# The experts' low-rank tile in four matmuls of 128 stationary columns, made one expert ahead

## What is computed

```python
xt = einsum('bct,bcd->bdt', x, cond_w[itok])               # 1024 tokens x 256
probs = softmax(xt @ gate_w); top_p, top_i = top_k(probs, 2)
for each of the two choices, each of 8 experts with at most 160 tokens per choice:
    h = gelu(buf @ w1[e] + b1[e])                          # 256 -> 1024
    y = h @ w2[e] + b2[e]                                  # 1024 -> 256
    y = y + gelu(buf @ wd[e]) @ wu[e]                      # the low-rank path, 256 -> 32 -> 256
    out[token] += y * weight
shared = gelu(xt @ sw1 + sb1) @ sw2 + sb2 + gelu(xt @ swd) @ swu
return x + out + 0.2 * shared
```

## Time and profile before

| what | us |
|---|---|
| median of the timed runs (3) | 177.4 |
| lowest and highest of them | 177.09 and 178.9 |
| the profiled execution, its own time | 177.45 |
| its span from the first to the last instruction | 175.6 |
| PE busy in the span | 169.9 |
| ACT busy | 140.5 |
| DVE busy | 144.1 |
| POOL busy | 96.8 |

### The profile page before, as it was taken

How to read it: one execution, slowest core, us unless ns; L and a number is a source line. 1 busy time by engine, 2 the same in 40 slices (tenths; PEclk the granted TensorE clock), 3 DMA queues, 4 the chain that set the end, 5 groups by cost and what they waited for, 6 DMA issues and landing times.

```text
span 175.6 us, 4118 instructions
## 1 busy us (share of the span) xinstructions
PE 169.9 (97%) x1442; PEld 164.3 (94%) x1442; DVE 144.1 (82%) x330; ACT 140.5 (80%) x315; POOL 96.8 (55%) x112
## 2 busy tenths in 40 slices
PE   5799999999999999999999999999999999999994
PEld 5666879999999999999999999999999999999993
DVE  3478999998695889989889699798988989889722
ACT  3277789407888998997899799999899999897920
POOL 5835348511547572097678858868837555074700
PEclk9999999999999999999999999999999999999999
DMA  4599100069929484595987768769778598776242
GB/s 127 163 350 349 41 2 4 7 175 299 362 56 318 103 304 111 194 252 79 307 252 117 275 193 157 213 197 234 194 255 185 144 312 164 247 247 78 30 90 67
DMA packets 25981, 31.84 MB, mean 181 GB/s; under 512 B 4668, under 2 KB 22488, under 8 KB 25960
## 3 DMA queue, kind: packets, MB, share of 16 engines
q1 hardware_dynamic: 21816, 26.22, 46.7%
q0 software_dynamic: 3904, 5.25, 17.0%
q10 hardware_dynamic: 240, 0.10, 0.2%
HBM read 26.31 MB, written 5.24 MB: 180 GB/s over the span
## 4 chain that ended last, share of the span: by engine, by line
PE 93%; DMA 5%; SPq 0%; DVE 0%; issue 0%; DVEq 0%
PE y_ps L1056 14%; PE y_ps L1057 14%; PE y_ps L1058 14%; PE hid_ps L1056 10%; PE hid_ps L1057 10%; PE hid_ps L1058 10%; DMA x_in<-in_x 5%; PE turn_ps L1056 4%; PE turn_ps L1058 4%; PE turn_ps L1057 4%; PE turn_ps L1235 3%; PE row_ps L1251 1%; PE hid_ps L1095 1%; PE y_ps L1195 1%; PE y_ps L1215 1%; PE y_ps L1251 0%
## 5 line engine op out<-in xcount | busy, mean ns | idle before, releaser
L495 POOL DMA_INDIRECT out_rows<-y_row,slot_tok x23 | 38.5, 1675 | 26.8 <-DVE y_row L946 11.6
L481 POOL DMA_INDIRECT slot_in<-slot_rows,slot_src x23 | 29.5, 1281 | 17.0 <-issue 6.1
L1056 PE MATMUL y_ps<-w_h,hid_h 128*128 128x256 f32 (+2 forms) x128 | 36.4, 285 | 0.0
L1057 PE MATMUL y_ps<-w_l,hid_h 128*128 128x256 f32 (+2 forms) x128 | 36.1, 282 | 0.0
L1058 PE MATMUL y_ps<-w_h,hid_l 128*128 128x256 f32 (+2 forms) x128 | 36.1, 282 | 0.0
L741 DVE TENSOR_TENSOR hid_l<-gelu_f,hid_h 128x320 fp32r<-128x320 f32 (+3 forms) x54 | 26.5, 500 | 8.0 <-ACT hid_h L643 7.5
L1056 PE MATMUL hid_ps<-xs_h,w_h 128*128 128x248 f32 (+6 forms) x96 | 27.6, 288 | 0.0
L1058 PE MATMUL hid_ps<-xs_h,w_l 128*128 128x248 f32 (+6 forms) x96 | 27.2, 284 | 0.0
L1057 PE MATMUL hid_ps<-xs_l,w_h 128*128 128x248 f32 (+6 forms) x96 | 27.2, 284 | 0.0
L718 DVE TENSOR_TENSOR w_l<-w_raw,w_h 128x512 fp32r<-128x512 f32 x40 | 26.7, 703 | 0.0
L643 ACT ACTIVATE hid_h<-hid_ps,bias_s 128x320 fp32r<-128x320 f32 (+2 forms) x48 | 26.4, 549 | 0.0
(11 more groups left out here) (260 smaller groups left out, 465.9 us busy)
## 6 DMA issues: line engine op xcount, KB each, us to landing
w_raw<-in_L_ffn_w SPq DMA_DIRECT2D x16, 1024.0 KB
w_raw<-in_L_ffn_sw SPq DMA_DIRECT2D x3, 1024.0 KB
x_in<-in_x SPq DMA_DIRECT2D x2, 512.0 KB, 4.1
w_raw<-in_L_ffn_sw SPq DMA_DIRECT2D x2, 512.0 KB, 6.5
slot_rows<-token_row SPq DMA_DIRECT2D x8, 128.0 KB, 5.1
wu_raw<-in_L_ffn_wu SPq DMA_DIRECT2D x24, 32.0 KB
out_rows<-base SPq DMA_DIRECT2D x1, 512.0 KB
slot_in<-slot_rows,slot_src POOLq DMA_INDIRECT x23
```

What stands on the lines that cost most here:

```text
L481: pool.indirect_dma_start(out=slot_in[par][0:n, s, :], out_offset=None, in_=x_rows, in_offset=bass.IndirectOffsetOnAxis(ap=slot_src[0:n, e ...
L495: pool.indirect_dma_start(out=out, out_offset=bass.IndirectOffsetOnAxis(ap=slot_tok[0:n, e, s:s + 1].bitcast(U32), axis=0), in_=y_row[0:n, ...
L1056: pe.matmul(out_ap, l_h, r_h, start=start, stop=False)
L1057: pe.matmul(out_ap, l_h, r_l, start=False, stop=False)
```

## The change

The low-rank tile leaves the hidden tiles of the experts (those of the shared expert stay as they were). `low_tile(e)` makes it in four matmuls: the stationary operand is 128 columns wide, two copies of the high part of `wd` and two of its low part, and both parts of the slots are streamed past it. Its 128 output rows hold the high products (rows 0 to 63) and the low products (64 to 127), which are still to be added. ACT copies the lower half to SBUF (`low_copy`), DVE adds the two (`low_sum`), ACT takes two gelus of the sum (`low_gelu_part`), DVE subtracts (`low_lo`).

The tile of expert e + 1 is made in period e, in PE's second pass of the second layer, ahead of feature tile 3 (`LOW_MADE_AT`); that of expert 0 at the start of period 0. ACT has the copy ahead of w2 chunk 2 (`LOW_COPY_AT`) and the gelus ahead of w2 chunk 3; DVE has the sum between w2 chunks 0 and 1 and the last subtraction after w2 chunk 2. The wait for `slots_lo` of the next expert moves from the head of the next period to `low_tile`. The two copies of `slots_hi_part` become one over both banks, as do the two subtractions of `slots_lo_part`. POOL makes the high part of `wd` ahead of the gather instead of after it, and waits for `low_made` there.

```diff
+LOW_COPY_AT = 2
+LOW_MADE_AT = 3
...
-        wd_h = [sb(f"wd_h{i}", [P, KD, 3, RANK], F32R) for i in range(2)]
-        wd_l = [sb(f"wd_l{i}", [P, KD, 3, RANK], F32R) for i in range(2)]
+        wd_s = [sb(f"wd_s{i}", [P, KD, 4, RANK], F32R) for i in range(2)]
...
+        low_sums = gelu_f[0:2 * RANK, 0:2, SLOTS:SLOTS + SLOTS // 2]
+        low_g = cond_g[0:RANK, :].rearrange("p (i n) -> p i n", i=2)[:, :, SLOTS:SLOTS + SLOTS // 2]
...
             def wd_hi_part(v, par):
-                if v >= 2:
-                    pool.wait_ge(hid_made, hid_before(v))
+                if v >= 3:
+                    pool.wait_ge(low_made, v - 2)
...
             def period(e, par):                                  # POOL
+                if e + 2 <= E:
+                    wd_hi_part(e + 2, par)
                 if e + 2 < E:
                     gather(e + 2, par)
-                if e + 2 <= E:
-                    wd_hi_part(e + 2, par)
...
+            def low_copy(e):
+                act.wait_ge(low_made, e + 1)
+                act.activation(low_sums, halves(turn_ps[0][2 * RANK:4 * RANK, 0:SLOTS]), ACT.Copy).then_inc(low_copied, 1)
+            def low_gelu_part(e):
+                act.wait_ge(low_summed, e + 1)
+                if e > 0:
+                    act.wait_ge(low_used, e)
+                    act.wait_ge(low_split, e)
+                act.activation(low_g, low_sums[0:RANK, :, :], ACT.Gelu)
+                act.activation(halves(low_s[0:2 * RANK, 0:SLOTS]), low_sums, ACT.Gelu).then_inc(low_gelu, 1)
...
             def slots_hi_part(n):
-                for k in range(KD):
-                    act.activation(xs_h[:, k, 0:n], turn_ps[k][:, 0:n], ACT.Copy).then_inc(slots_hi, 1)
+                act.activation(xs_h[:, :, 0:n], turn_both[:, :, 0:n], ACT.Copy).then_inc(slots_hi, 1)
...
             def period(e, par):                                  # ACT
-                for j in range(HT):
+                if e == 0:
+                    low_copy(0)
+                for j in range(1, HT):
                     gelu_tile(e + 2, j, MOST[e], lambda f: bias_s[:, e, f:f + 1])
+                    if e == 0 and j == 1:
+                        low_gelu_part(0)
...
                 for c in range(CHUNKS):
+                    if c == LOW_COPY_AT and e < E - 1:
+                        low_copy(e + 1)
+                    if c == CHUNKS - 1 and e < E - 1:
+                        low_gelu_part(e + 1)
                     w2_chunk(e + 2, par, c)
...
+            def low_sum(e):
+                dve.wait_ge(low_copied, e + 1)
+                dve.tensor_tensor(low_sums, halves(turn_ps[0][0:2 * RANK, 0:SLOTS]), low_sums, ALU.add).then_inc(low_summed, 1)
+            def low_lo(e):
+                dve.wait_ge(low_gelu, e + 1)
+                dve.tensor_tensor(halves(low_s[2 * RANK:LOW, 0:SLOTS]), low_g, halves(low_s[0:RANK, 0:SLOTS].bitcast(F32)),
+                                  ALU.subtract).then_inc(low_split, 1)
...
                 for c in range(CHUNKS - LATE_LO):                # DVE
+                    if c == LOW_COPY_AT - 1 and e < E - 1:
+                        low_sum(e + 1)
                     w2_chunk(c, par, e + 2)
+                if e < E - 1:
+                    low_lo(e + 1)
...
+            def low_tile(e, par, size):
+                pe.wait_ge(slots_lo, e + 1)
+                pe.wait_ge(wd_lo, e + 2)
+                for k in range(KD):
+                    both = wd_s[par][:, k, :, :].rearrange("p g r -> p (g r)")
+                    pe.matmul(turn_ps[0][:, 0:size], both, xs_h[:, k, 0:size], start=(k == 0), stop=False)
+                    ins = pe.matmul(turn_ps[0][:, 0:size], both, xs_l[:, k, 0:size], start=False, stop=(k == KD - 1))
+                ins.then_inc(low_made, 1)
...
                 for f in range(NF):                              # expert_out, and rows_out likewise
+                    if m == KD - 1 and f == LOW_MADE_AT:
+                        midway()
...
                 for e, size in enumerate(sizes):                 # experts
-                    pe.wait_ge(slots_lo, (e + 1) * KD)
-                    for j in range(HT):
+                    if e == 0:
+                        low_tile(0, other, size)
+                    for j in range(1, HT):
                         hidden(e + 2, j, other, e + 1, xs_h, xs_l, slice(0, size), size)
```

More of the change, by code:

```diff
@@ L84, in build @@
         y_ps = [bank(f"y_ps{i}") for i in range(2)]
-        turn_ps = [bank(f"turn_ps{i}") for i in range(2)]
+        turn_both = ctx.enter_context(nc.psum_tensor("turn_both", [P, KD, 512], F32))
+        turn_ps = [turn_both[:, k, :] for k in range(KD)]
         row_ps = bank("row_ps")
@@ L249, in build @@
         wu_lo = sem("wu_lo")
+        low_made = sem("low_made")
+        low_copied = sem("low_copied")
+        low_summed = sem("low_summed")
+        low_gelu = sem("low_gelu")
+        low_split = sem("low_split")
+        low_used = sem("low_used")
         hid_made = sem("hid_made")
@@ L334, in held_by @@
         def held_by(u, j):
-            tiles = [i for i in range(1 if u == LAST else 0, j) if hid_banks(u)[i] is hid_banks(u)[j]]
+            tiles = [i for i in range(0 if u < 2 else 1, j) if hid_banks(u)[i] is hid_banks(u)[j]]
             return tiles[-1] if tiles else None
@@ L921, in slots_lo_part @@
                 n = MOST[e]
[L922 to L925, removed]
+                dve.wait_ge(slots_hi, e + 1)
+                dve.tensor_tensor(xs_l[:, :, 0:n], turn_both[:, :, 0:n], xs_h[:, :, 0:n].bitcast(F32),
+                                  ALU.subtract).then_inc(slots_lo, 1)
             def weigh_rows(e, par):
@@ L1193, in expert_out @@
                 cols = slice(m * P, (m + 1) * P)
-                pe.wait_ge(hid_split, hid_count(e + 2, 0))
-                pe.matmul(dst, wu_s[par][:, cols], low_s[:, 0:size], start=True, stop=False)
+                pe.wait_ge(low_split, e + 1)
+                ins = pe.matmul(dst, wu_s[par][:, cols], low_s[:, 0:size], start=True, stop=False)
+                if m == KD - 1:
+                    ins.then_inc(low_used, 1)
                 for f in range(NF):
+                    if m == KD - 1 and f == LOW_MADE_AT:
+                        midway()
                     if m == 0:
@@ L1201, in expert_out, with rows_out @@
                 ins.then_inc(y_made, 1)
-            def rows_out(e, par, size):
+            def rows_out(e, par, size, midway):
                 v = e + 1
@@ L1214, in rows_out @@
                     cols = slice(s * P, s * P + n)
-                    pe.matmul(dst, low_s[:, cols], wu_s[par][:, :], start=True, stop=False)
+                    ins = pe.matmul(dst, low_s[:, cols], wu_s[par][:, :], start=True, stop=False)
+                    if s == tiles[-1]:
+                        ins.then_inc(low_used, 1)
                     for f in range(NF):
+                        if s == tiles[-1] and f == LOW_MADE_AT:
+                            midway()
                         if s == tiles[0]:
```

41 lines of the change are left out of this document (23 added, 18 removed).

## The result

The changed kernel takes 182.97 us in the median of four runs (182.04 to 185.47), the kernel before, beside it, 177.45: a ratio of 1.028 (1.018 to 1.037). It is slower, as forecast, and 182.0 was the forecast. One of the four runs, 185.47, is a slow one, and the ratio leaves it out. The profiled execution took 182.25 us with a span of 180.3, for 175.6 before: 4.7 us more.

The account below looks back on a forecast made before the run. PE was taken as the bound, busy 169.9 of 175.6 us, but the round through ACT and DVE would outlast its period. Waits of 6.46 less 1.92 for fewer matmuls add 4.54 to 177.45: 182.0 us, range 178.4 to 184.2.

Parts of the forecast that it names:

- waits forecast: PE's waits per period, for the next slots at `low_tile` and for ACT's copies at the transposes; sum 6.46 us.
- 1.92: PE's gain in us: six matmuls become four for eight experts, 16 fewer at 0.12 us each.
- The signs: PE idle before transposes (1.9 us in period 1, 0.2 after) and `low_tile` (0.4 to 1.1); ACT idle before new gelus.
- The wide operand: `low_tile`'s four matmuls with 128 stationary columns instead of 96 should cost the same 0.12 us each.
- The round of 3.52 us: From slots ready through DVE's sum, ACT's gelus and w2 chunk 3 to next gelu 1: 3.52 us; least trusted step.
- Period 0: `sort_biases` delays DVE's sum; PE waits 0.41 us for slots ready at 66.0, then 1.85 for results in period 1.
- Period 7: The last period loses six matmuls and is 0.72 us shorter, with no wait forecast.
- One copy for two saves nothing: Merged copy in `slots_hi_part`: no fixed part saved on ACT, 1.0 ns a column either way.
- POOL's `wd` first costs nothing: POOL making `wd` ahead of the gather is free: its slots are wanted only in period 2, past 85 us.
- A: Rival: PE is the bound and every wait stays covered, so faster, 175.5 us; chance 0.10.
- B: Rival: ACT never gets late, only 3.0 us of waits for the slots remain, 178.5 us; chance 0.10.
- C: Rival: period 1's 1.85 us of idle PE lets the granted clock fall, 185.6 us; chance 0.06.

Follow-up runs that it names:

- e10: e6 with the transposes of the results one hidden tile later (behind tile 3 instead of 2): 177.63 us, 0.996 of the kernel before.
- e1: Changed kernel with DVE's low-rank sum right behind w1 chunk 3, ahead of `sort_biases` and w2 chunk 0: 180.36 us, 1.0095 of the kernel before.
- 2: Changed kernel with the next slots ahead of w1 on ACT and DVE: 182.41 us, 1.020 of the kernel before.
- e9: Changed kernel with the transposes of the results behind hidden tile 3 instead of 2: 182.34 us, 1.028 of the kernel before.
- e6: e3 with DVE's low part of `wd` also ahead of the slots: 178.37 us, 0.994 of the kernel before.
- e7: e6 with POOL's gather ahead of `wd`'s high part again: 178.42 us, 0.995 of the kernel before.
- e3: Changed kernel with both the sum ahead of the w2 chunks and the slots ahead of w1: 179.33 us, 1.001 of the kernel before.
- e5: Changed kernel with `sort_biases` behind DVE's w2 chunks of period 0: 181.47 us, 1.017 of the kernel before.
- e12: e10 with hidden-tile gelus and subtractions only on the columns the matmuls use: 177.18 us, 0.990 of the kernel before.
- e4: Control: the kernel before the change with the slots ahead of w1: 178.03 us, 0.998 of the kernel before.
- e8: e7 with six matmuls instead of four for each low-rank tile: 177.73 us, 0.997 of the kernel before.

## Why the prediction was right

**The size.** 182.0 forecast for 182.25 of the profiled execution. By periods, each as the change of its length with the matmuls it lost or gained taken out (0.24; +0.24 in period 0), from the stretches shown and the earlier trace rows:

| period | waits forecast | measured |
|---|---|---|
| 0 | 0.41 | 0.04 |
| 1 | 2.45 | 2.36 |
| 2 | 0.22 | 0.04 |
| 3 | 0.74 | 0.73 |
| 4 | 0.95 | 0.91 |
| 5 | 1.09 | 1.16 |
| 6 | 0.60 | 0.74 |
| 7 | 0 | 0.53 |
| sum | 6.46 | 6.51 |

6.51 - 1.92 = 4.59, against the stretch's 4.58. That the totals agree within 0.05 is partly luck: periods 0 to 2 were forecast 0.64 us too long, and period 7 got 0.53 that was not forecast.

**The signs.** ACT's idle time before its new gelus was 2.04 us in period 0 and 0.42 to 0.47 after. PE's at `low_tile` was 0.30 to 0.64 us in five periods (forecast 0.4 to 1.1 in six). At the transposes PE waited in period 1 alone to speak of; in periods 3 and 4 they started 0.13 and 0.24 late (100.56 to 100.81, 114.69 to 115.05, less a step of 0.12).

**The wide operand** cost no more, as assumed: in e10, in period 2, where `low_tile` does not wait, the four matmuls of 264 columns start at 94.07, 94.19, 94.31 and 94.43, steps of 0.12 as with 96 stationary columns.

**The round of 3.52 us** was the step trusted least. From the end of the slots to the sum 110.95 to 112.66, 1.71 (forecast 1.72); from there to the gelus 113.18, 0.52 (0.48 + 0.03); the two gelus 0.74 by the next starts in period 0, 69.26 to 70.00 (0.77); w2 chunk 3 0.64, 70.00 to 70.64 (0.52); together 3.61. The copies of the results 0.65 (0.64). The one term that was off is w2 chunk 3: the price of a chunk in a row of chunks was taken, and alone behind the gelus it took 0.12 more (124.53 to 125.17 in e10 as well); why was not tried. Experiment 1 shows that the round is the cause of most of the loss (3.48 of 4.58), and 2 and 9 that single waits are not: each took one away and found it again at the other place, with stretches of 124.49 and 124.17 for 124.23.

**Period 0** was wrong in detail. The slots were ready at 65.40 (64.58 + 0.82), not at 66.0, because ACT ran some 0.5 us earlier there than the prediction let it; PE asked at 65.45 and did not wait. The same head start made the results' wait 1.38 (1.55 in starts, 1.68 less a step of 0.13) instead of 1.85. Period 1's total still came out, because the later waits took up the rest.

**Period 7** was forecast to get its full 0.72 and got 0.19, 11.66 for 11.85: with six matmuls fewer ahead of the same work PE came too early for DVE's weighing of rows (0.24 in starts at 159.78; the rest lies in smaller steps that were not traced). No step of the prediction looked there.

**"One copy for two saves nothing"** was nearly right. ACT's merged copy took its turn in 0.58 us (next starts, 94.33 to 94.91) where the pair took 0.64, and DVE's in 0.73 (110.13 to 110.86) where the pair took 0.80: 0.06 and 0.07 us a period. By the Trainium skill's fixed part for ScalarE ("VectorE: DVE Perf Modes", the TRN2 errata) ACT's merge would save 0.14, an estimate; the 0.06 measured is less than half of it. (Over seven periods that estimate is 1.0, not the prediction's 0.9; its sum did not use it.)

**"POOL's `wd` first costs nothing"**: by e6 and e7 no difference was found.

**The rivals.** A, PE stays the bound, would have needed the round shortened: no version here reached its 175.5 in the median, and even without waits of 0.3 us and more the 16 matmuls brought 0.59 of 1.92 (e10). The Trainium skill's rule in "Perfetto Trace Analysis" (Identifying the Most-Contended Engine), to optimize the engine of highest occupancy first, would have led to A. It was not enough here: PE was that engine before (97% of the span) and after (95%), and with 16 matmuls fewer the kernel was slower, since the added hand-overs made the round longer than PE's period. B came about when the sum was moved (e1). C did not: the granted clock is 1.00 in each stretch of the changed kernel, period 1 with its 1.38 us of idle PE among them.

## What to carry to other kernels

Where one engine looks like the bound, write down for its neighbours the loop that a tile goes through (from the first gelu to the slots, the sum, and back to the next gelu) and compare its length with the period; a change that adds a link to it costs its excess once a period, at whatever wait happens to stand last. Do not chase the wait that shows: shorten the loop, and the wait does not come back at another place. And before counting on fewer matmuls, look in each period for the engine that is second: if it has next to nothing to spare, it cannot make up for a late load, and the gain is given back there.

## What the runs showed that was not expected

A wait costs PE more than its idle time. In period 5 the wait shown is 0.64 us, but from the last matmul before it to the second one behind it (starts at 137.85, 138.76 and 138.98) pass 1.13 us instead of two steps of 0.115: 0.90 us lost. The first matmul after the wait is 0.38 long, for 0.28 of the others, and holds its follower for 0.22.

Loads of w2 came late in most of the versions (ACT waited 1.47 us in e3, 1.84 in e5, 0.96 in e6, 1.50 in e7, 1.85 in e12), and not in the profiles of the kernel before, the changed one, e4, e8 or e9. Being faster is not what they share: e5 is as slow as the changed kernel, and e8 is not. Which queue or transfer the loads collide with was not tried.

ACT's gelus have a fixed part that its copies hardly show: 0.41 us a step at 320 columns and 0.36 at 256 (163.52 to 163.88 in e12), an eighth less time for a fifth fewer columns.
